# Sums between the first scores and the products in a step of the second context attention

## The reference

```
q = (query @ Wq)   # 256 x 1024, 32 heads of 32
k = (key @ Wk)     # 4096 x 256,  8 key/value heads of 32
v = (value @ Wv)
k, v = repeat(k, 4), repeat(v, 4)
scores = einsum('bhqd,bhkd->bhqk', q, k) * 32 ** -0.5
probs = softmax(scores)
out = einsum('bhqk,bhkd->bhqd', probs, v)
return out.reshape(...) @ Wo
```

## Time and profile before

| | us |
|---|---|
| median of 3 runs | 2177.09 (2160.72 to 2186.52) |
| profiled execution | 2171.91 |
| its span, first to last instruction | 2170.6 |
| TensorE busy in the span | 1951.5 (90%) |
| VectorE, ScalarE, GpSimd busy | 1349.7, 857.8, 533.0 |
| mean granted clock of TensorE | 0.948 of 2.4 GHz |

### The profile page before, as it was taken

How to read it: one execution, slowest core, us unless ns; L and a number is a source line. 1 busy time by engine, 2 the same in 40 slices (tenths; PEclk the granted TensorE clock), 3 DMA queues, 4 the chain that set the end, 5 groups by cost and what they waited for, 6 DMA issues and landing times.

```text
span 2170.6 us, 29653 instructions
## 1 busy us (share of the span) xinstructions
PE 1951.5 (90%) x11932; PEld 1416.9 (65%) x11932; DVE 1349.7 (62%) x1654; ACT 857.8 (40%) x1401; POOL 533.0 (25%) x248
## 2 busy tenths in 40 slices
PE   7899999999998999999998976798988999978977
PEld 5799999999996878786777854332322222356843
DVE  3444545445445787889667645667777776466465
ACT  2211111111105666665644520355655656635421
POOL 0000000000003555554300000255655666510000
PEclk9999999999998999999999997798999999989889
DMA  4543433433228666656454355221424320036042
GB/s 170 166 122 95 124 103 102 122 95 105 73 79 234 197 198 191 202 198 207 141 148 142 108 121 155 68 66 44 90 67 86 76 56 1 21 121 227 1 182 73
DMA packets 154808, 259.30 MB, mean 119 GB/s; under 512 B 36477, under 2 KB 102321, under 8 KB 147505
## 3 DMA queue, kind: packets, MB, share of 16 engines
q1 hardware_dynamic: 154673, 257.42, 39.7%
HBM read 192.39 MB, written 61.76 MB: 117 GB/s over the span
## 4 chain that ended last, share of the span: by engine, by line
PE 77%; DVE 12%; ACT 4%; issue 4%; DMA 2%; SPq 0%; ACTq 0%; DVEq 0%
PE psum L468 10%; PE psum L1695 7%; PE psum L1712 5%; PE psum L449 4%; PE psum L451 4%; PE psum L450 4%; PE psum L436 3%; PE psum L278 3%; PE psum L279 3%; PE psum L280 3%; DVE top L1870 3%; PE psum L1728 3%; PE psum L809 3%; PE psum L416 2%; PE psum L1676 2%
## 5 line engine op out<-in xcount | busy, mean ns | idle before, releaser
L1870 DVE TENSOR_REDUCE top<-psum 128x4 f32<-128x2048 f32 x128 | 293.2, 2290 | 131.4 <-PE psum L1676 130.8
L1946 POOL TENSOR_TENSOR added<-probs_f 128x1024 f32<-128x1024 f32 x126 | 299.7, 2379 | 277.7 <-ACT probs_f L1805 166.4
L1805 ACT ACTIVATE probs_f<-psum 128x512 f32<-128x512 f32 x512 | 278.0, 595 | 206.2 <-PE psum L1695 204.9
L601 DVE TENSOR_REDUCE top<-psum 128x2 f32<-128x512 f32 x272 | 186.5, 692 | 198.0 <-PE psum L436 198.0
L900 DVE TENSOR_TENSOR probs_low<-probs,probs_high 128x1024 fp32r<-128x1024 f32 x136 | 192.6, 1421 | 77.8 <-ACT probs L863 77.5
L1695 PE MATMUL psum<-q_rows,k_rows 97*128 97x512 f32 x512 | 206.6, 483 | 3.9 <-DMA q_rows<-t_high 3.1
L1695 PEld LDWEIGHTS psum<-q_rows,k_rows 97*128 97x128 f32 x512 | 84.2, 201 | 189.5 <-ACT probs_f L1805 152.6
L862 ACT ACTIVATE probs_high<-psum 128x1024 fp32r<-128x1024 f32 x136 | 139.9, 1028 | 162.4 <-PE psum L811 149.1
L449 PE MATMUL psum<-c_high,w_high 128*128 128x256 f32 (+1 forms) x672 | 190.6, 284 | 3.2 <-issue 3.2
L450 PE MATMUL psum<-c_low,w_high 128*128 128x256 f32 (+1 forms) x672 | 190.6, 284 | 0.0
L451 PE MATMUL psum<-c_high,w_low 128*128 128x256 f32 (+1 forms) x672 | 190.5, 284 | 0.0
(11 more groups left out here) (356 smaller groups left out, 3867.3 us busy)
## 6 DMA issues: line engine op xcount, KB each, us to landing
wf_rows<-in_ffn_w_dram SPq DMA_DIRECT2D x42, 512.0 KB, 4.2
staged<-in_ctxT_dram SPq DMA_DIRECT2D x32, 512.0 KB, 4.6
k_four<-k_high SPq DMA_DIRECT2D x128, 128.0 KB, 2.9
wf_rows<-in_ffn_w_dram SPq DMA_DIRECT2D x8, 1376.0 KB, 8.3
q_dram<-wf_turned SPq DMA_DIRECT2D x42, 256.0 KB, 2.3
gate_up<-q_dram SPq DMA_DIRECT2D x10, 1024.0 KB, 8.0
value_high<-v_high SPq DMA_DIRECT2D x32, 256.0 KB, 3.6
value_low<-v_low SPq DMA_DIRECT2D x32, 256.0 KB, 4.4
```

The lines of the kernel that those rows point to most:

```text
L601: dve.tensor_reduce(top0[:, r0:r0 + 2, n], psum[:, bank, :].rearrange("p (i n) -> p i n", i=2), AX_X, ALU.max).then_inc(*b.bank_read.up())
L1805: act.activation(probs[:, n % 6, half * BANK:(half + 1) * BANK], psum[:, half, :], ACT.Exp, scale=scale).then_inc(*f.exped.up())
L1870: dve.tensor_reduce(top1[:, :, t, chunk], psum[:, MAXIMA:MAXIMA + G1, :], AX_X, ALU.max).then_inc(*f.max_read.up())
L1946: pool.tensor_tensor(added[pair % 4][:], probs[:, n % 6, :], probs[:, (n + 1) % 6, :], ALU.add).then_inc(*f.added.up())
```

## The change

The sum group leaves the end of the step and is issued in the following step, between the scores A and the products. It begins at step 3 of the first head instead of step 2, and the last group follows behind the loop. No instruction is added or removed, and nothing on another engine changes.

```diff
--- before.py
+++ after.py
@@ -1774,6 +1774,8 @@
                     kv, p = divmod(pair, PER)
                     if pair + 1 < PAIRS:
                         scores(2 * pair + 2)
+                    if pair >= 3:
+                        sum_up((pair - 1) // 2 - 1, (pair - 1) % 2)
                     weigh(pair)
                     if pair + 1 < PAIRS:
                         scores(2 * pair + 3)
@@ -1781,8 +1783,7 @@
                         turn_tops(kv + 1)
                     while quads < quads_by(pair):
                         maxima()
-                    if pair >= 2:
-                        sum_up(pair // 2 - 1, pair % 2)
+                sum_up(PAIRS // 2 - 2, 1)
                 sum_tiles(PAIRS - 2)
                 sum_tiles(PAIRS - 1)
                 oT = [(oT_high[:, kv, :], oT_low[:, kv, :], f.o_split.at(4 * kv + 4)) for kv in range(KV1)]
```

## The result

| | before | after |
|---|---|---|
| median of 20 runs | 2170.34 us | 2190.32 us |
| lowest to highest | 2157.02 to 2195.99 | 2184.16 to 2202.39 |
| profiled execution | 2171.91 | 2194.98 |
| stage, first to last score matmul | 505.0 | 522.1 |

The ratio is 1.0094 with a 95% interval of 1.0068 to 1.0119: on 2170 us that is +20.4 us, between +14.8 and +25.8. The kernel got slower by just under 1%. The forecast was +25.8 us and 2198. The measured +0.94% falls into the class "within 1%", to which the prediction gave 0.36, and not into "slower by over 1%", to which it gave 0.58; the interval reaches over that line, to 1.19%.

A forecast was written before the change was run, and what follows sets the result against it. TensorE bounds regular steps, with ScalarE's 1.27 us return loop just fitting; the move makes its intervals unequal. 13.8 + 2.1 + 2.7 + 7.2 = +25.8 us on the profiled 2171.9 gives 2198; range 2174 to 2221.

The forecast's parts named there:

- The loop: Regular steps: ScalarE's return needs 1.27 us from second scores to next A; A to second scores 2.34; step +0.28.
- Last steps: Stage's end, without maxima: 17 steps at 3.61 us each, +6.8 us, and the last A to second scores +0.43.
- head 6: Its steps 0 to 12, by the same prices as a full head: +2.1 us.
- Head 0: From its step 3, by the same prices, with two double-maximum steps at about +0.2 each: +2.7 us.
- Heads 1 to 5: Full heads of 16 steps at +2.76 us each: +13.8 us.
- 0 to 2 and 8 to 12: Per head, seven regular steps +1.96 us and step 2, no longer waiting for VectorE, -0.14; five heads +9.1.
- 3 to 7: Per head +0.68 us before and -0.39 after VectorE's chain, which hides moved work between: together +0.29.
- 13 to 15: Per head +0.19 us at the turned maxima's copy, then +0.05, then +0.41 with ScalarE's copy; five heads +3.3.
- mode-switch rival: Whole stage: array mode switches decide, each step 0.14 us shorter, 17.6 us saved, 2154 us; chance 0.08.
- clock rivals: Stage's clock: a quarter of the lower clock goes, 2187 us, chance 0.25; or gaps lower it, 2218, chance 0.07.
- Nothing happens: VectorE sets the stage's end, so the time stays 2172 us; chance 0.05.

The follow-up runs named there:

- Experiments 1: Changed kernel with the moved sums one place later, behind the products and before the second scores; 2196.15 us, ratio 1.0088 to the kernel before.
- 2: Kernel before with the maxima, instead of the sums, moved between A and the products; 2186.37 us, ratio 1.0058.
- 4: Kernel before, old order, each exponential cut to 256 of its 512 columns; 2151.91 us, ratio 0.9922.
- experiment 5: Changed order with each exponential cut to 256 of its 512 columns; 2134.68 us, ratio 0.9839 to the kernel before.
- experiment 6: Kernel before, old order, GpSimd's additions cut to 64 of 1024 columns; 2146.97 us, ratio 0.9896.

## Why the prediction was right, and where it was not

**The loop.** Right, and to the hundredth: 2.34 and 1.27 were forecast from the last steps of before and the sums behind products; measured 2.34 and 1.27. The last hundredths are luck: sums to products took 0.46 where 0.43 was forecast, and products to B 0.97 for 1.00. Experiments 1, 2, 4 and 5 show the mechanism from several sides.

**Last steps.** +6.8 us and 0.43 forecast. From A of step 112 to A of step 126 the profile gives 45.19 and 50.50, +5.3, for 14 of the 17 steps; head 6 with the first three of them +4.6. Head 6 and the last steps together: forecast 2.1 + 7.2 = 9.3, measured 4.6 + 5.3 + 0.4 = 10.3. **Head 0:** forecast 2.7, measured 2.8, but by chance: 0.85 lie in steps 0 to 2, where nothing had been forecast, and step 14 is 1.4 shorter, which makes up for several steps that are longer than forecast.

**Heads 1 to 5.** Forecast +13.8, measured +4.0; here lies the whole error. Split by steps, summed over the five heads from the starts of A:

| steps | forecast | measured |
|---|---|---|
| 0 to 2 and 8 to 12 | +9.1 | +9.3 |
| 3 to 7 | +1.5 | -4.9 |
| 13 to 15 | +3.3 | -0.5 |

*Steps 3 to 7.* The step "VectorE's chain sets the maxima of steps 5 and 6, moved work is hidden there: 0" took VectorE's chain as fixed. It is not. In head 3 of the changed kernel (VectorE's line is now 1893, GpSimd's 1947):

```profile
1609.33 4.90 POOL L1947 TENSOR_TENSOR added<-probs_f 128x1024 f32<-128x1024 f32 x2 [2.45 <-ACT probs_f L1806]
...
1611.50 3.01 DVE L1893 TENSOR_TENSOR inverse_f<-odd_f,inverse_f 32x256 f32<-32x256 f32 x2
...
1616.86 0.80 PE L1676 MATMUL psum<-k_four,q_nat_high 32*128 32x512 f32 x4 [2.57 <-DVE top L1871]
...
1618.48 0.75 DVE L1893 TENSOR_TENSOR inverse_f<-odd_f,inverse_f 32x256 f32<-32x256 f32 x2
...
1619.99 2.36 POOL L1947 TENSOR_TENSOR added<-probs_f 128x1024 f32<-128x1024 f32 x1 [5.76 <-PE psum L1728]
...
1622.61 0.75 PE L1676 MATMUL psum<-k_four,q_nat_high 32*128 32x512 f32 x4
```

The second block's two multiplications take 0.75 us together, while GpSimd has been idle for 5.76 us, waiting for sums that now come a step later; the maxima of step 6 (1622.61) then wait for nothing, where before they waited 2.04. TensorE was itself slow here, which took up some of the wait; the windows view of this stretch has a clock of 0.50:

```profile
1617.00:1623.00 6.00, 6.00 (x28) 2.04 (x28) 5.80 (x8) 1.72 (x4) 2.36 (x1) 0.50 0.00 0
```

Step 6 as a whole took 5.71 us for 6.99 before. The prediction had asked of GpSimd's additions only whether they would be late, and put them at nothing; it had not asked where they would fall. In head 5 both blocks meet an addition:

```profile
1741.74 3.01 DVE L1893 TENSOR_TENSOR inverse_f<-odd_f,inverse_f 32x256 f32<-32x256 f32 x2
...
1747.10 0.51 PE L1676 MATMUL psum<-k_four,q_nat_high 32*128 32x512 f32 x4 [2.57 <-DVE top L1871]
...
1748.73 2.92 DVE L1893 TENSOR_TENSOR inverse_f<-odd_f,inverse_f 32x256 f32<-32x256 f32 x2
1749.01 4.84 POOL L1947 TENSOR_TENSOR added<-probs_f 128x1024 f32<-128x1024 f32 x2 [4.54 <-PE psum L1728]
...
1754.04 0.80 PE L1676 MATMUL psum<-k_four,q_nat_high 32*128 32x512 f32 x4 [3.67 <-DVE top L1871]
```

3.01 and 2.92 us, and 3.67 us of waiting at the maxima of step 6. So heads 2 to 4 gained 1.3 to 2.2 us in these steps and heads 5 and 6 lost 1.1 each: which of them meet is a matter of phase. That the additions stretch VectorE is shown by experiment 6; that just these coincidences make the 6.4 us between forecast and measurement is only read from one profile, and the lower clock in the same steps has a share that is not separated.

*Steps 13 to 15.* Head 1 alone gives -2.5: before, its step 14 and 15 ran partly at the lower clock, after not. The others are at +0.35 to +0.6, near the forecast of 0.65. I had counted the clock at these steps as unchanged. Nothing ties this to the move: in number 1, with the same intervals, other heads escape the lower clock at step 14.

**The rivals.** The mode-switch rival was wrong for this kernel since its condition (exponential back in under 1.10) does not hold, and right in kind where experiment 5 makes it hold (1.05): 0.14 per regular step and a turned sign. That 17.2 us stand beside the 17.6 worked out for it is partly chance, since the last steps lose 0.29 each (2.89 to 3.18) and steps 3 to 7 gain more than 0.14. By the Trainium skill, "TensorEngine Tiling (Array Packing)", Key Properties, changing the tiling mode drains the engine, so the move should save one drain per step; the trace agrees as soon as nothing else binds: 3.33 to 3.19, the same 0.14 by which the sums were shorter beside the products. The clock rivals: the stage's clock is 0.92 for 0.91, so neither a penalty nor a quarter back is seen. The first wait did get shorter, 2.57 us in heads 3 and 5 for 3.05, as that rival had said, and the lower level followed it all the same. "Nothing happens" falls.

**The number.** 2190.3 lies in the range of 2174 to 2221, but a range of 47 us is wide for an effect of 20. Against the ratio the forecast of 25.8 us is at the upper end of the interval, too large by 5.4 us, and against the one profiled stage it is too large by 8.7 (17.1 against 25.8): heads 1 to 5 are 9.8 below the forecast, the rest 1.1 above it. The cause, the bound of 1.27 us, is shown; the size for the whole kernel held only because the stage's other errors stayed smaller than the effect.

## What to carry to other kernels

When two engines hand buffers back and forth twice per step, the order of the fillers is a budget: each interval must be at least the other engine's return time, and total work that fits says nothing if it is divided unevenly. Reading the return time where it binds alone (here the last steps without maxima) prices the reordering before it is made. And a wait in which moved work is "hidden" may move itself: ask what its length depends on, and test the chain of waits with an experiment before believing the engine that it names.

## What the runs showed of the hardware

VectorE's operations on two operands in SBUF are held up while GpSimd adds: 32 x 256 multiplications of 0.41 us last up to 2.6 us, 13 of 32 over 1 us in the kernel before and 10 of 32 after; with GpSimd's additions cut to 64 of 1024 columns none is longer than 0.55. The first multiplication within head 3 in the kernel before, and the addition that started 0.05 us ahead of it:

```profile
1601.49 2.60 DVE L1892 TENSOR_TENSOR inverse_f<-odd_f,inverse_f 32x256 f32<-32x256 f32 x1
1601.44 2.38 POOL L1946 TENSOR_TENSOR added<-probs_f 128x1024 f32<-128x1024 f32 x1 [0.82 <-ACT probs_f L1805]
```

The addition ends at 1603.82, the multiplication 0.28 us later. So do all that were held up: each of the 13 of before and of the 10 of after ends 0.27 to 0.29 us behind the end of an addition. The maximum reductions, which read PSUM, kept 2.27 to 2.30 us in all 128 cases of before, 98 of which overlap an addition. The transposes of the inversion, with one operand in SBUF, kept 0.69 to 0.70, the 17 that overlap an addition too. The Trainium skill, "SBUF — State Buffer", section "SBUF: two separate sides", describes the port pair that both engines use as an exclusive lock held for a whole instruction, also for VectorE operations with two SBUF inputs against a GpSimd operation that reads SBUF; the durations here, up to the length of one addition (2.4 us) more, and the ends at 0.28 us behind the addition agree with that.
